# A four-layer graph network on one core: 482 scatters of layer 0's edge pass wait for the batches of the pass

## The chip, the cores and the metric

The kernel runs on one core of one Trainium2 chip. The metric is the device time in microseconds of one execution, the median of several runs. TensorE (PE) has two clock levels, 1.2 and 2.4 GHz; the profile shows the granted clock of a stretch as a share of the higher one. GpSimd is called POOL, VectorE DVE, ScalarE ACT, SyncE SP.

## The reference

A graph of 12,500 nodes and 200,000 edges (sorted by destination `dst`), 128 features, goes through four layers, each on the normalised and rectified output of the one before. Cut to what matters here:

```python
# layer 0: sum of the edge features per destination node, then a two-layer network
recv_agg = segment_sum(edge_attr_128, dst)
x = x + relu(concat(recv_agg, h, u) @ W1 + b1) @ W2 + b2
# layer 1: attention over the incoming edges; s_rel needs a score of every edge
s_rel = (edge_attr_128 @ w_r.T) @ att_w[256:384]
# layer 2: sums over edges in both directions: by col (= dst) and by row (= src)
agg_fwd = segment_sum(w * x[col], row);  agg_bwd = segment_sum(w * x[row], col)
# layer 3: weighted mean over incoming edges, linear maps, layer norm
```

The sums by `src` in layer 2 need the edges in another order, which the kernel works out itself in its first 900 us. A table of keys in device memory (`keyd`) belongs to this order, and is first read back at L2349, in a phase that comes after layer 1.

## The kernel before

The program is a row of phases. Each phase has a block of code for each of the five engines; inside a phase the engines run freely and wait for each other only at semaphores, and all meet at the end of it. Every engine works through its own block strictly in order. The change is in the phase `p_l0` (L1244), layer 0.

**The edge pass.** `edge_pass` (L984) goes over the edges in NR = 391 batches of 512 edges, unrolled by six. For each batch:

- SP loads the batch's edge features, 256 KB, into one of six slots of `XR` (`load_ea`, L1176). The load for batch b waits until `bd` has reached b - 3.
- DVE makes a one-hot selection matrix from the batch's keys (L1005), semaphore `oh`. Then it adds the finished sums of the batch two before into `AREA` (L1044); for this it waits for PE by the semaphore `mmd`. Then it takes the scores of the batch: four products of the edge features with a fixed vector (L1077). The first of the four raises the semaphore `bd` by one. The phase's `bd` is thus the count of batches whose scores have begun.
- PE multiplies features by the selection matrix (L1106, four f32 products that the profile lists as eight matmuls), waits for ACT's copy (`ohb`), counts the edges with four small bf16 matmuls (L1111), and the last of these raises `mmd`.
- ACT copies the selection matrix to bf16 for the count (L1145). It has one buffer for this, so it waits for PE's `mmd` of the batch before. Then it writes the scores of the batch (L1157).

So `mmd` is the one signal from PE on which both ACT and DVE depend in every batch.

```python
i.then_inc(mmd, 1)                            # PE, unit(): i is the last L1111 of the batch
e.wait_ge(mmd, k + 1)                         # ACT, again(s), ahead of L1145
e.wait_ge(mmd, n_mm if ends else n_mm + 2)    # DVE, accumulate(), ahead of L1044
```

**The scatters.** POOL has nothing to do in the edge pass itself. Its block in this phase writes `keyd`: NBP = 482 indirect DMAs (L1256), each of which scatters 128 rows of five numbers from SBUF to rows in device memory. Twelve semaphores `sc` take turns, so at most twelve scatters are on their way at once. Behind them in POOL's queue come the wait for the end of the edge pass (`edone`), two memsets (L1260, L1261) and the additions of the node stage.

Layers 1, 2 and 3 have edge passes as well, in which POOL gathers rows by indirect DMAs (L1214, L1237). Those of layers 2 and 3 use the same `edge_pass` without counts and scores; a gather there waits for the same kind of semaphore `bd` (L1234), here raised by a small memset of DVE (L1047) once PE's `mmd` has come, and may run up to nine batches ahead.

Of the kernel before, what the change touches and what calls it, by code (L numbers as in the profile page):

```python
# [24 lines left out]
def gnn(nc, x, src, dst, ea, ew, u, W1, b1, W2, b2, w, w_r, att, loop_w, Ws, bs, Wd, bd_,  # L25
# [3 lines left out]
    NR = NBF + 1  # L29
# [16 lines left out]
    NBP = 4 * (NCK - 1) + NBT  # L46
# [1129 lines left out]
    def load_ea(p, bd, off=2):  # L1176

        ready = [p.sem(f"ea{s}") for s in range(UN)]

        @p.on("sync")  # L1180
        def _(e):
            v = ea[0:NBF * BE, :].rearrange("(b p r) f -> b p (r f)", p=128, r=4)
            t = ea[NBF * BE:NE, :].rearrange("(p r) f -> p (r f)", r=4)

            def one(b, s):
                e.dma_start(XR[:, s * BE:(s + 1) * BE], v[bass.ds(b, 1)].rearrange("b p k -> (b p) k")).then_inc(ready[s], 16)
            for s in range(UN):
                one(s, s)
            if NIT > 1:
                with e.Fori(1, NIT) as it:  # L1190
                    for s in range(UN):

                        e.wait_ge(bd, (it - 1) * UN + (s + off))
                        one(it * UN + s, s)
            e.wait_ge(bd, (NIT - 1) * UN + off)
            e.dma_start(XR[0:TP, 0:BE], t).then_inc(ready[0], 16)
            for s in range(UN):
                e.wait_ge(ready[s], 16 * (NIT + (s == 0)))
        return ready
# [44 lines left out]
    def p_l0():  # L1244
        p = Phase()
        ready = load_ea(p, p.sem("bd"), 3)
        edge_pass(p, NR, TP, 48, 0, KLD, lambda s: EA[:, s], ready, 16, AB[:, 0, :], count=True, srel=True)
        sc = [p.sem(f"sc{i}") for i in range(12)]

        @p.on("gpsimd")  # L1250
        def _(e):

            for b in range(NBP):
                if b >= 12:
                    e.wait_ge(sc[b % 12], 16 * (b // 12))
                e.indirect_dma_start(keyd, bass.IndirectOffsetOnAxis(ap=SI[:, b:b + 1].bitcast(U32), axis=0),  # L1256
                                     MP[:, 5 * b:5 * b + 5], None).then_inc(sc[b % 12], 16)

            e.wait_ge(p.sem("edone"), 1)
            e.memset(R[32:33, :], M0).then_inc(p.sem("mi"), 1)  # L1260
            e.memset(R[64:65, :], 0.0).then_inc(p.sem("mi"), 1)  # L1261
            e.wait_ge(p.sem("mi"), 2)
            for i in range(12):
                e.wait_ge(sc[i], 16 * ((NBP - 1 - i) // 12 + 1))
        l0_nodes(p)
        p.run()
# [1652 lines left out]
```

## Time and profile before

| | us |
|---|---|
| median of 3 runs | 9834.15 (9824.49 to 9837.78) |
| span of the profiled execution, first to last instruction | 9823.1 |
| layer 0's edge pass: POOL's first scatter starts | 907.76 |
| ... DVE's first batch (L1005) | 923.41 |
| ... POOL's last scatter starts | 1555.80 |
| ... DVE's end signal (L1088) | 2229.64 |

The profiled execution is known by its span; the median of the runs is 11.0 us above it, for what lies around the first and the last instruction and for the spread of the runs.

In the rows further down, a line of a timeline is: start in us, duration in us, engine, source line, operation, what is written and read, how many instructions are merged, and in brackets how long the engine had been idle and what released it. "issue" means nothing that the profile shows; "remote" stands where the profile finds no instruction of this core whose end would have been the release. A line of windows is: the stretch, its length, then for PE, PE's weight loads, DVE, ACT and POOL the busy time and the number of instructions, the granted clock of TensorE, the busy share of the DMA engines and GB/s.

### The profile page before, as it was taken

What the parts mean: (1) busy time and instruction counts of PE and PEld (TensorE: products, weight loads), DVE (VectorE), ACT (ScalarE), POOL (GpSimd) and SP (SyncE); (2) the same over time, 40 slices, a digit from 0 to 9 for tenths busy, and PEclk for the clock granted to TensorE, in tenths of its full rate; (3) what the DMA queues carried; (4) which work ended last, traced back from release to release, by engine and by line L of the source; (5) the groups of instructions that cost most, each with busy time, mean ns of one, the idle gap of its engine ahead of it and who ended that gap; (6) DMA issues with size and microseconds to landing.
All of it is one profiled execution on the core that took longest, in us unless ns stands there. A gap on an engine that the chain in (4) does not pass through costs nothing. (4 is left out here: it accounts for less than half of the span.)

```text
span 9823.1 us, 218886 instructions
## 1 busy us (share of the span) xinstructions
PE 7099.9 (72%) x59894; PEld 6078.6 (62%) x59895; DVE 6196.8 (63%) x20052; ACT 3293.8 (34%) x9071; POOL 4369.4 (44%) x5518
## 2 busy tenths in 40 slices
PE   5943004778967878878878797777797777696777
PEld 5843004765656666666657676667696766696666
DVE  7997004883346666666667676555786556786556
ACT  4722001333432222222223452000560002667785
POOL 0002772001036666666663355566465553465661
PEclk8955557999976666666667899888898887898987
DMA  0001003551123333333333586556686554686553
GB/s 21 2 2 29 10 9 87 150 149 46 38 59 87 86 86 85 87 86 88 87 85 115 198 287 215 164 166 161 245 338 186 164 163 134 253 338 183 166 166 117
DMA packets 640399, 1262.17 MB, mean 128 GB/s; under 512 B 121108, under 2 KB 179132, under 8 KB 639896
## 3 DMA queue, kind: packets, MB, share of 16 engines
q1 hardware_dynamic: 418919, 704.46, 21.3%
q0 software_dynamic: 199040, 544.46, 20.1%
q10 hardware_dynamic: 22196, 10.20, 0.4%
q8 instruction: 129, 2.11, 0.1%
q14 instruction: 115, 0.94, 0.0%
HBM read 780.96 MB, written 477.75 MB: 128 GB/s over the span
## 5 line engine op out<-in xcount | busy, mean ns | idle before, releaser
L1214 POOL DMA_INDIRECT GS<-t1d,KI x1564 | 1479.9, 946 | 1000.3 <-issue 380.3
L1106 PE MATMUL PS<-w,GS 128*128 128x128 f32 x6128 | 902.9, 313 | 319.2 <-DVE w L1005 251.4
L1106 PE MATMUL PS<-w,AREA 128*128 128x128 f32 x6048 | 860.6, 306 | 334.8 <-DVE w L1005 291.1
L1106 PEld LDWEIGHTS PS<-w,GS 128*128 128x128 f32 x6128 | 850.3, 223 | 371.7 <-DVE w L1005 294.1
L1106 PEld LDWEIGHTS PS<-w,AREA 128*128 128x128 f32 x6048 | 808.5, 215 | 385.2 <-DVE w L1005 333.5
L1005 DVE TENSOR_TENSOR w<-PS,KI 128x512 f32<-128x512 f32 x964 | 666.5, 691 | 316.9 <-issue 306.7
L2547 PE MATMUL PS<-AREA 128*128 128x128 bf16 x13392 | 842.7, 220 | 8.4 <-ACT GS L2473 4.6
L2547 PEld LDWEIGHTS PS<-AREA 128*128 128x128 bf16 x13392 | 792.0, 98 | 79.3 <-issue 6.1
L2522 DVE TENSOR_SCALAR AREA<-PS,w 128x1024 bf16<-128x1024 bf16 x558 | 715.9, 1284 | 161.2 <-PE PS L2533 161.2
L2491 POOL TENSOR_TENSOR AREA<-AREA,w 128x192 int32<-128x192 int32 x1116 | 528.3, 504 | 473.1 <-PE PS L2547 296.8
L2473 ACT ACTIVATE GS<-PS 128x1024 f32<-128x1024 f32 x558 | 571.3, 1024 | 315.2 <-PE PS L2547 300.0
L1715 PE MATMUL PS<-w,XR 128*128 128x128 f32 x3128 | 671.8, 381 | 0.0
L1663 ACT ACTIVATE w<-PS,w 128x48 f32<-128x48 f32 x1564 | 341.5, 301 | 941.5 <-PE PS L1658 474.9
L1709 PE MATMUL PS<-w,GS 128*128 128x128 f32 x3128 | 631.4, 370 | 0.0
L1106 PE MATMUL PS<-w,XR 128*128 128x128 f32 x3128 | 508.4, 313 | 165.6 <-DVE w L1005 152.9
L1715 PEld LDWEIGHTS PS<-w,XR 128*128 128x128 f32 x3128 | 577.5, 277 | 56.8 <-issue 45.5
L1237 POOL DMA_INDIRECT GS<-xbuf,KI x484 | 462.6, 956 | 334.0 <-DVE w L1047 226.5
L1709 PEld LDWEIGHTS PS<-w,GS 128*128 128x128 f32 x3128 | 607.5, 287 | 0.7
L1237 POOL DMA_INDIRECT AREA<-xbuf,KI x480 | 458.5, 955 | 303.1 <-DVE w L1047 217.3
L1256 POOL DMA_INDIRECT keyd<-AREA x482 | 487.1, 1011 | 194.0 <-issue 161.9
L1106 PEld LDWEIGHTS PS<-w,XR 128*128 128x128 f32 x3128 | 433.5, 215 | 198.8 <-DVE w L1005 181.7
L1111 PE MATMUL PS<-w,ONB 128*128 128x48 bf16 x1564 | 107.6, 189 | 596.1 <-issue 564.9
(431 smaller groups left out, 14522.1 us busy)
## 6 DMA issues: line engine op xcount, KB each, us to landing
xbuf<-GS SPq DMA_DIRECT2D x558, 512.0 KB
XR<-in_edge_attr SPq DMA_DIRECT2D x780, 256.0 KB
pbuf<-AREA SPq DMA_DIRECT2D x482, 256.0 KB
GS<-t1d,KI POOLq DMA_INDIRECT x1564
AREA<-t2d ACTq DMA_DIRECT2D x121, 64.0 KB
GS<-xbuf,KI POOLq DMA_INDIRECT x484
keyd<-AREA POOLq DMA_INDIRECT x482
AREA<-xbuf,KI POOLq DMA_INDIRECT x480
```

The source lines that it names most:

```text
L1005: return e.tensor_tensor(SEL[s % 3], num.unsqueeze(1).to_broadcast([128, 4, width]), kl.unsqueeze(2).to_broadcast([128, 4, width]), ALU.is ...
L1106: i = e.matmul(PS[:, s % 3, 0:128], feats(s)[0:m, r, 0:D], SELW[s % 3][0:m, width * r:width * r + 128], start=(r == 0), stop=(r == 3))
L1214: e.indirect_dma_start(GS[0:m, s, r, 0:wide], None, table, bass.IndirectOffsetOnAxis(ap=idx[0:m, c:c + 1].bitcast(U32), axis=0)).then_inc( ...
L1237: e.indirect_dma_start(gslot(s), None, buf, bass.IndirectOffsetOnAxis(ap=idx[:, b:b + 1].bitcast(U32), axis=0)).then_inc(ready[s], 16)
L1256: e.indirect_dma_start(keyd, bass.IndirectOffsetOnAxis(ap=SI[:, b:b + 1].bitcast(U32), axis=0), MP[:, 5 * b:5 * b + 5], None).then_inc(sc[ ...
L1663: n = e.activation(U1[i][:, r, :], uv(i)[:, r, :], ACT.Identity, bias=ZC[i][:, r:r + 1])
L1709: n = e.matmul(PS[:, 4 + i, 0:128], GS[0:m, s, r, 0:D], LLW[l][0:m, WD * r:WD * r + 128], start=(r == 0), stop=(r == 3))
L1715: n = e.matmul(PS[:, 4 + i, 128:256], EA[0:m, s, r, :], LLW[l][0:m, WD * r:WD * r + 128], start=(r == 0), stop=(r == 3))
L2473: e.activation(OUT[s % 3], PS[:, 3 + 2 * (s % 2):5 + 2 * (s % 2), :], ACT.Copy).then_inc(ev, 1)
L2491: e.tensor_tensor(WTI[s % UN], TABI[:, bass.ds(held[0][s], 192)], ZI[:, 0:1].to_broadcast([128, 192]), ALU.add).then_inc(wt, 1)
L2522: e.tensor_scalar(OHT[s % 3], PS[:, s % 3, :].bitcast(BF16).rearrange("n (k d) -> n d k", d=2), IPB[:, 0:1], None, ALU.is_equal).then_inc( ...
L2547: i = e.matmul(PS[:, 3 + 2 * (s % 2) + d, 128 * r:128 * r + 128], OHT[s % 3][:, d, 128 * r:128 * r + 128], WT[(2 * s + d) % UN][:, 128 * k ...
```

## The change

Each scatter gets one more wait. The scatter number b waits until `bd` has reached `b * 391 // 482`, which is until the scores of that many batches have begun. The first two scatters (b = 0, 1) wait for nothing, and the last one for 390. Between them each batch frees one scatter, and in 90 of the batches a second one. No instruction is added to any other engine, none is moved, and no DMA changes its size or target.

```diff
@@ -1253,6 +1253,8 @@
             for b in range(NBP):
                 if b >= 12:
                     e.wait_ge(sc[b % 12], 16 * (b // 12))
+                if b * NR // NBP:
+                    e.wait_ge(p.sem("bd"), b * NR // NBP)
                 e.indirect_dma_start(keyd, bass.IndirectOffsetOnAxis(ap=SI[:, b:b + 1].bitcast(U32), axis=0),
                                      MP[:, 5 * b:5 * b + 5], None).then_inc(sc[b % 12], 16)
```

## Rows read from the trace of the kernel before

**Rows 1.** The page, busy tenths in 40 slices of 245.6 us.
```profile
POOL 0002772001036666666663355566465553465661
PEclk8955557999976666666667899888898887898987
```

**Rows 2.** Windows, the edge pass of layer 0 in two stretches.
```profile
923.00:1577.00 654.00, 49.65 (x249) 41.60 (x249) 31.75 (x211) 9.25 (x40) 475.33 (x470) 0.50 0.07 10
1583.00:2229.00 646.00, 492.06 (x4431) 454.82 (x4428) 541.05 (x3689) 209.40 (x738) 0.00 (x0) 0.93 0.51 149
```

**Rows 3.** Groups of instructions, 1000 to 1500 us: count, busy, mean ns, idle before.
```profile
L1256 POOL DMA_INDIRECT keyd<-AREA x370 | 375.8, 1016 | 125.5 <-issue 125.5
...
L1077 DVE CUSTOM_DVE_ANT_0 w<-XR,AREA 128x128 f32<-128x128 f32 x60 | 14.0, 288 | 1.0
...
L1145 ACT ACTIVATE w<-w 128x192 bf16<-128x192 f32 x15 | 5.4, 363 | 497.1 <-remote 497.1
...
L1044 DVE TENSOR_TENSOR AREA<-AREA,PS 128x96 f32 x15 | 3.8, 255 | 476.8 <-remote 476.8
```

**Rows 4.** Timeline, one period of the slow stretch.
```profile
1008.13 0.36 ACT L1145 ACTIVATE w<-w 128x192 bf16<-128x192 f32 x1 [33.14 <-remote]
...
1008.55 0.34 PE L1111 MATMUL PS<-w,ONB 128*128 128x48 bf16 x4 [30.88 <-issue]
1009.21 2.05 PE L1106 MATMUL PS<-w,XR 128*128 128x128 f32 x8 [0.33 <-issue]
...
1041.73 0.36 ACT L1145 ACTIVATE w<-w 128x192 bf16<-128x192 f32 x1 [33.14 <-remote]
1041.83 0.26 DVE L1044 TENSOR_TENSOR AREA<-AREA,PS 128x96 f32 x1 [32.03 <-remote]
```

**Rows 5.** Timeline, ACT and PE at the start of the pass.
```profile
923.88 0.36 ACT L1145 ACTIVATE w<-w 128x192 bf16<-128x192 f32 x1 [5.89 <-DVE w L1005]
...
942.33 0.36 ACT L1145 ACTIVATE w<-w 128x192 bf16<-128x192 f32 x1 [16.93 <-remote]
```

**Rows 6.** Timeline, POOL and ACT where the scatters end.
```profile
1555.80 0.96 POOL L1256 DMA_INDIRECT keyd<-AREA  x1 [0.30 <-issue]
1577.23 0.36 ACT L1145 ACTIVATE w<-w 128x192 bf16<-128x192 f32 x1 [31.04 <-remote]
...
1582.34 0.36 ACT L1145 ACTIVATE w<-w 128x192 bf16<-128x192 f32 x1 [4.65 <-remote]
...
1583.13 0.36 ACT L1145 ACTIVATE w<-w 128x192 bf16<-128x192 f32 x1 [0.34 <-PE PS L1111]
```

**Rows 7.** Groups of instructions, 1583 to 2229 us.
```profile
L1106 PE MATMUL PS<-w,XR 128*128 128x128 f32 x2952 | 463.4, 305 | 153.9 <-DVE w L1005 152.3 <-issue 0.8
...
L1077 DVE CUSTOM_DVE_ANT_0 w<-XR,AREA 128x128 f32<-128x128 f32 x1476 | 342.8, 287 | 25.2
L1145 ACT ACTIVATE w<-w 128x192 bf16<-128x192 f32 x369 | 133.9, 363 | 177.4 <-DVE w L1005 117.5 <-PE PS L1111 57.7 <-issue 2.3
```

**Rows 8.** Timeline of layer 2's first edge pass, one hold of PE's signal.
```profile
6160.12 3.94 PE L1106 MATMUL PS<-w,AREA 128*128 128x128 f32 x32 [1.41 <-DVE w L1005]
...
6164.91 0.95 POOL L1237 DMA_INDIRECT AREA<-pbuf,XR  x1 [0.30 <-issue]
...
6167.08 0.06 DVE L1047 MEMSET w<- 1x1 f32 x1 [0.98 <-DMA GS<-t1d,KI]
```

**Rows 9.** Waits in that pass, 6020 to 6890 us: total, times, longest.
```profile
DVE w L1047 <- PE PS L1106: 152.7, 121, 2.4
```

**Rows 10.** Windows, the edge passes of layer 2 (two), 3 and 1.
```profile
6020.00:6890.00 870.00, 635.06 (x4407) 599.45 (x4405) 517.87 (x1649) 0.00 (x0) 521.57 (x546) 0.88 0.60 164
7370.00:8180.00 810.00, 587.99 (x4276) 553.53 (x4273) 481.40 (x1430) 22.52 (x22) 474.62 (x516) 0.86 0.58 170
8880.00:9640.00 760.00, 544.01 (x3836) 510.73 (x3837) 453.05 (x1445) 603.50 (x1907) 451.92 (x473) 0.89 0.58 164
2860.00:5240.00 2380.00, 1928.28 (x9669) 1483.37 (x9669) 1513.97 (x6568) 610.21 (x2709) 1454.99 (x1538) 0.66 0.33 86
```

## The prediction, made before the changed kernel ran

> **What bounds the kernel now.** I read four views, in this order.
>
> First the slices of the page [rows 1]. POOL is busy 7 tenths in two slices (at about 1000 to 1500 us) while the granted clock of PE stands at 0.5, and right after POOL falls silent the clock goes to 0.9. So something odd happens beside the scatters.
>
> Second the windows of the edge pass [rows 2]. In the 654 us that the scatters take, PE executes 249 instructions; in the 646 us behind it 4431. The groups say it in batches: L1145 runs once per batch, 15 times in 500 us [rows 3] and 369 times in 646 us [rows 7]. A batch takes 33.6 us beside the scatters and 646 / 369 = 1.751 us without them. Half of the pass goes by for 22 batches.
>
> Third, what the slow batches wait for. ACT (L1145) and DVE (L1044) are idle for 497 and 477 of 500 us, and the profile puts the release down to nothing on this core ("remote") [rows 3]. The timeline shows one period [rows 4]. PE's count matmuls of a batch (L1111) end at 1008.55 + 0.34 = 1008.89, PE then does the sums of the next batch, and stands from 1011.26. ACT starts only at 1041.73 and DVE at 1041.83. Both need the one signal that L1111 raises, `mmd`, so it reached them 1041.73 - 1008.89 = 32.84 us late. The period is constant (15 batches in 500 us, idle 33.14 before each). Signals in the other direction are prompt: L1145 starts at 1008.13 and lasts 0.36, PE's L1111 follows at 1008.55. I read this as: while POOL issues scatters without a pause, PE's completion signals are held back, and here they get out only after some 33 us.
>
> That POOL's stream is the cause rests on its two edges. The signals before the first batch pass (ACT at 923.88), at the second batch ACT is idle for 16.93 us [rows 5], and after the last scatter at 1555.80 there are two more late ones, 31.04 and 4.65, and from 1583.13 on none [rows 6].
>
> Fourth, the other edge passes, where POOL gathers and waits for `bd`, as the scatters will. There the signal is held too, but briefly. In layer 2, 32 matmuls (four batches) end at 6164.06; POOL's last gather of that run starts at 6164.91; DVE goes on at 6167.08 [rows 8], 3.0 us after PE's end and 2.17 us after POOL's last issue. POOL had run out of batches that it may gather for, paused, and the signal came out. The longest such wait of DVE for PE in 870 us is 2.4 us, in 121 waits [rows 9]; no 33 us anywhere.
>
> **The change, part by part.**
>
> *The waits themselves.* 480 of 482 scatters get a wait. It is on POOL, which has no other work here: what queues behind is the end of the pass (a memset of one row and the node stage's additions). POOL needs 0.96 + 0.30 = 1.26 us per scatter [rows 6], so 482 / 391 x 1.26 = 1.55 us per batch, less than the 1.751 of a batch: POOL keeps up, and the last scatter (wait for 390) starts one batch before the pass ends. At most the memset begins one scatter later, 1.3 us. The table is first read in a phase behind layer 1, so later scatters cost nobody.
>
> *What the spreading removes.* From DVE's first batch at 923.4 to its end signal at 2229.6 (both in the table of times) are 1306 us for 391 batches. Without any hold it would be 391 x 1.751 = 685 us. That is the most that can be won: 621 us. What is late next is then DVE itself, busy 541 of 646 us [rows 2].
>
> *What the spreading brings.* The scatters now run beside all batches instead of 22. I price three things.
> - Holds of PE's signal. Bounded below by nothing: a batch frees one or two scatters, never four in a row as in rows 8. Bounded above by a full hold in every batch: scores begin, POOL issues, 2.17 us later the signal comes out [rows 8], and about 0.8 us pass until the next scores begin (ACT 0.36, DVE's addition, the first score). That is 3.0 us per batch, 1.2 more than 1.751. The nearest rows are the three passes of layers 2 and 3 [rows 10], with one gather per batch and the same kind of wait. A batch is eight matmuls there: 870 us / 551 = 1.58 us, of which PE is busy 635 / 551 = 1.15, excess 0.43; 810 / 535 = 1.515 against 1.10, excess 0.415; 760 / 480 = 1.585 against 1.135, excess 0.45. I take 0.43 us per batch on top of 1.751, which gives 2.18, times 391 = 852 us. It is an analogy: there the bound is PE, here DVE, and POOL may run further ahead there but needs one DMA per batch against 1.23 here.
> - DMA traffic. The scatters move with 10 GB/s beside loads at 149 GB/s, and the engines' share is 0.07 against 0.51 [rows 2]. SP loads three batches ahead. I cost it at 0; if that cover were gone, it would be at most the 0.07 of 685 us, 48 us.
> - DVE beside POOL. L1077 takes 288 ns beside scatters [rows 3] and 287 without [rows 7]: 0.
>
> The page "SBUF — State Buffer" of the Trainium skill, section "Who interferes with whom", speaks against the change: a DVE instruction with two inputs in SBUF (L1077 is one) and a GpSimd instruction that reads SBUF exclude each other for their whole length. By that rule a scatter would stop the scores. The trace does not agree: 288 against 287 ns. What it would give is the fourth rival.
>
> *The clock.* In the slow stretch it is 0.50, in the fast one 0.93 [rows 2], with PE waiting between batches in both. With short holds I expect 0.8 to 0.9, as in layers 2 and 3 [rows 10]. PE is busy 492 / 369 = 1.33 us per batch at 0.93 [rows 2, 7]; at 0.85 that is 1.46, under DVE's 1.751, and the clock costs nothing. Were it 0.5 throughout, PE would need 2.05 + 0.34 + 0.33 = 2.72 us per batch [rows 4].
>
> *Sum.* 852 - 1306 = -454 us. Against the profiled execution 9823.1 - 454 = 9369; the median lies 11 us above the span, so 9834 - 454 = 9380 us.
>
> **The rivals.**
> 1. *No holds to speak of.* For it: at most two scatters follow each other. Against: 1.26 us issue and 2.17 us until a hold ends overlap from batch to batch at 1.75 us, so POOL's stream may count as unbroken. 9834 - 621 = 9213 us.
> 2. *A hold in every batch, or PE at half clock.* For it: layer 1, with four gathers per batch, has clock 0.66 [rows 10]. Against: layers 2 and 3. 391 x 2.72 to 3.0 = 1064 to 1173 us, so 9592 to 9701 us.
> 3. *The long hold stays (slower).* The place is the same signal, the price some 33.6 us each time. For it: after the last scatter POOL was silent, and still the signal took until 1577.23 and the next until 1582.34 [rows 6]; a pause alone did not free it. The scatters go to device memory and the gathers of layers 1 to 3 come from it, so these may be no guide. It becomes slower than before from (1306 - 685) / 31.8 = 20 long holds on; with one in every batch the pass would take 391 x 33.6 = 13138 us and the kernel about 21670. Against: the first batch passed with a dozen scatters on their way [rows 5], and after a release only one or two scatters follow.
> 4. *DVE and POOL exclude each other.* 482 x 0.958 us = 462 us of scatters on top of 685 us: 1147 us, 9675 us. Against: 288 and 287 ns.
> 5. *The scatters are not the cause* and a slow start stays for another reason: 9834 us. Against: both edges of rows 5 and 6.
>
> The Trainium skill, "DMA: Bandwidth & Descriptors", section "Anatomy of one DMA", says that a DMA's completion can take long above all when it writes to device memory, as the scatters do. No row here shows a scatter's completion. By it a hold would last longer than 2.17 us, which leans to the second rival.
>
> **How the numbers follow.** Forecast, short holds (1.85 to 2.6 us per batch): 0.56. Rival 1: 0.24. Rival 2: 0.11. Rival 3: 0.04. Rival 4: 0.02. Rival 5: 0.03. The forecast's own range is 391 x 1.85 = 723 to 391 x 2.6 = 1017 us, 9251 to 9545. For 8 in 10 I add rival 1 on the low side, down to 9200, and a little of rival 2, up to 9560. A measurement of this kernel tells 0.2% (20 us) from no change. Faster than that are the forecast and rivals 1, 2 and 4: 0.93. The same is rival 5: 0.03. Slower is rival 3: 0.04.
>
> **What would show it.** In the changed profile: no "remote" wait of about 33 us before L1145 and L1044; the pass ends at about 923 + 852 = 1775 us on DVE's end signal; L1256 spread over all of it, its idle time now released by DVE's L1077; ACT's L1145 with waits of 1 to 3 us for PE's L1111, some 100 to 250 of them; clock of the pass 0.8 or more. Rival 1: hardly any such wait and an end near 1610. Rival 2: L1106 at 2.05 us per eight matmuls and clock 0.5. Rival 4: L1077 longer than 290 ns. I am wrong if waits of 30 us stay in number, or if the phases behind layer 0 change by more than the spread of the runs, 13 us.

## The result, and the profile after

The changed kernel takes 9416.92 us (median of 4 runs, 9400.87 to 9427.75) against 9829.32 us of the kernel before in the same comparison: ratio 0.9585, 95% interval 0.9572 to 0.9598. The forecast was 9380 us: 454 us less than before, measured 412. The profiled execution has a span of 9399.2 us, 423.9 less than before.

In the changed kernel all lines behind the edit have moved by two: the scatter is L1258, POOL's memsets are L1262 and L1263. DVE's end signal (L1088) comes at 1816.0 us instead of 2229.6. That is 413.6 of the 423.9 us; the node stage gives 3.2 (layer 1's first gather at 2816.8 before, 2400.0 after) and the rest of the kernel 7.1, which is within the spread of the runs.

The page of the changed kernel, the same two rows as [rows 1], each slice now 235 us:

```profile
POOL 0000555400466666666633556654655551556561
PEclk8965877799666666666678998888998886998887
```

The peak of 7 tenths is gone: the scatters lie over three slices at 5 tenths and one at 4, and the granted clock there is 0.7 to 0.8 instead of 0.5.

Windows of the changed kernel, the whole pass and the node stage with the start of the next phase, to be set against [rows 2]:

```profile
923.00:1816.00 893.00, 619.13 (x4692) 571.56 (x4692) 577.01 (x3913) 193.43 (x782) 468.36 (x480) 0.79 0.47 116
1816.00:2400.00 584.00, 534.39 (x2522) 347.01 (x2522) 192.61 (x1040) 222.37 (x452) 53.03 (x28) 0.95 0.13 35
```

One stretch replaces two. 893 us for 391 batches are 2.28 us each; before, most of the first 22 took 33.6 each and the rest 1.751.

Groups of the changed kernel, 923 to 1816 us, to be set against [rows 3, 7]:

```profile
L1106 PE MATMUL PS<-w,XR 128*128 128x128 f32 x3128 | 578.1, 345 | 118.1 <-DVE AREA L1044 53.2 <-issue 47.2 <-DVE w L1005 14.6
...
L1258 POOL DMA_INDIRECT keyd<-AREA x480 | 468.4, 976 | 432.9 <-DVE w L1077 290.8 <-issue 142.2
...
L1077 DVE CUSTOM_DVE_ANT_0 w<-XR,AREA 128x128 f32<-128x128 f32 x1564 | 363.8, 288 | 26.6
L1145 ACT ACTIVATE w<-w 128x192 bf16<-128x192 f32 x391 | 141.8, 363 | 645.4 <-remote 283.9 <-PE PS L1111 256.0 <-DVE w L1005 76.8
```

POOL is now released by DVE's scores (L1077), as the edit says. L1077 itself lasts 288 ns as before. ACT's idle time is still the largest and still ends with PE's signal, "remote" or L1111. How it is cut up, the waits of the same stretch show (total, times, longest):

```profile
POOL keyd L1258 <- DVE w L1077: 290.8, 149, 14.4
ACT w L1145 <- remote: 283.9, 86, 4.3
ACT w L1145 <- PE PS L1111: 256.0, 229, 2.8
```

No wait of ACT for PE's signal is longer than 4.3 us, where they were 33.14 [rows 4]. The timeline of the changed kernel shows one of the long ones:

```profile
1499.41 0.96 POOL L1258 DMA_INDIRECT keyd<-AREA  x1 [0.30 <-issue]
1500.67 0.96 POOL L1258 DMA_INDIRECT keyd<-AREA  x1 [0.30 <-issue]
1501.02 0.37 PE L1111 MATMUL PS<-w,ONB 128*128 128x48 bf16 x4
1501.93 0.96 POOL L1258 DMA_INDIRECT keyd<-AREA  x1 [0.30 <-issue]
1503.87 0.36 ACT L1145 ACTIVATE w<-w 128x192 bf16<-128x192 f32 x1 [4.02 <-remote]
...
1505.35 0.98 POOL L1258 DMA_INDIRECT keyd<-AREA  x1 [2.46 <-DVE w L1077]
```

PE's last count matmul, which raises `mmd`, ended at 1501.39, inside a run of scatters 1.26 us apart. ACT goes on at 1503.87, 1.94 us after the start of the last of them. The stalled batch had left POOL without a scatter that it might issue, until 1505.35. So the hold starves the stream that causes it, and ends.

### The profile page after: what moved, and what is told of

Same layout as the page of the kernel before. It is cut to its first block and busy times, and to the rows that moved or that the text cites. A ratio compares the mean times of both kernels' runs of the same rounds, so it can differ in the third digit from the quotient of the medians.

```text
span 9399.2 us, 219356 instructions
## 1 busy us (share of the span) xinstructions
PE 7177.7 (76%) x59894; PEld 6153.7 (65%) x59895; DVE 6200.2 (66%) x20052; ACT 3266.3 (35%) x9071; POOL 4357.1 (46%) x5518
## 5 line engine op out<-in xcount | busy, mean ns | idle before, releaser
L1106 PE MATMUL PS<-w,GS 128*128 128x128 f32 x6128 | 882.1, 308 | 333.9 <-DVE w L1005 277.3
L1106 PE MATMUL PS<-w,AREA 128*128 128x128 f32 x6048 | 884.6, 312 | 317.4 <-DVE w L1005 257.4
L1106 PEld LDWEIGHTS PS<-w,GS 128*128 128x128 f32 x6128 | 828.9, 218 | 386.2 <-DVE w L1005 320.4
L1106 PEld LDWEIGHTS PS<-w,AREA 128*128 128x128 f32 x6048 | 832.8, 221 | 368.6 <-DVE w L1005 297.9
L1005 DVE TENSOR_TENSOR w<-PS,KI 128x512 f32<-128x512 f32 x964 | 666.6, 691 | 318.0 <-issue 307.4
L1258 POOL DMA_INDIRECT keyd<-AREA x482 | 470.5, 976 | 465.4 <-DVE w L1077 290.8
L1717 PE MATMUL PS<-w,XR 128*128 128x128 f32 x3128 | 674.9, 383 | 0.0
L1106 PE MATMUL PS<-w,XR 128*128 128x128 f32 x3128 | 578.1, 345 | 118.1 <-DVE AREA L1044 53.2
L1711 PE MATMUL PS<-w,GS 128*128 128x128 f32 x3128 | 631.4, 370 | 0.0
L1717 PEld LDWEIGHTS PS<-w,XR 128*128 128x128 f32 x3128 | 580.2, 278 | 57.5 <-issue 46.8
L1711 PEld LDWEIGHTS PS<-w,GS 128*128 128x128 f32 x3128 | 608.4, 287 | 0.5
L1106 PEld LDWEIGHTS PS<-w,XR 128*128 128x128 f32 x3128 | 507.1, 246 | 135.8 <-DVE w L1005 72.4
L1005 DVE TENSOR_TENSOR w<-PS,XR 128x512 f32<-128x512 f32 x558 | 385.9, 692 | 179.6 <-issue 174.4
```

The costliest lines, as they stand in the source:

```text
L1005: return e.tensor_tensor(SEL[s % 3], num.unsqueeze(1).to_broadcast([128, 4, width]), kl.unsqueeze(2).to_broadcast([128, 4, width]), ALU.is ...
L1106: i = e.matmul(PS[:, s % 3, 0:128], feats(s)[0:m, r, 0:D], SELW[s % 3][0:m, width * r:width * r + 128], start=(r == 0), stop=(r == 3))
L1711: n = e.matmul(PS[:, 4 + i, 0:128], GS[0:m, s, r, 0:D], LLW[l][0:m, WD * r:WD * r + 128], start=(r == 0), stop=(r == 3))
L1717: n = e.matmul(PS[:, 4 + i, 128:256], EA[0:m, s, r, :], LLW[l][0:m, WD * r:WD * r + 128], start=(r == 0), stop=(r == 3))
```

## The experiments

Twelve runs in five sessions after that of the result, and the sessions turned out not to be alike. The kernel before, run in each of them, took 8269, 8265, 9829, 9904 and 9834 us. In the first two no recorded signal `mmd` of layer 0's pass is more than 0.02 us behind the end of its matmul, in the other three many are. I call them sessions without and with holds. The two profiles of this case belong to the second kind. The record gives a chip number for each session: 11, 2, 2, 13 and 12. The same number, 2, stands for one without holds and, a quarter of an hour later, for one with them, so, if the number means one chip, it is a state rather than a fixed trait; what sets it is not known. Every run on record has a granted clock, which is read from the profiler's records, so none tells whether holds occur without that recording.

### First session (without holds): four kernels

**All scatters behind the node stage.** The loop of scatters is moved to the end of the phase.

```diff
+            e.wait_ge(p.sem("edone"), 1)
+            e.memset(R[32:33, :], M0).then_inc(p.sem("mi"), 1)
+            e.memset(R[64:65, :], 0.0).then_inc(p.sem("mi"), 1)
+            e.wait_ge(p.sem("mi"), 2)
+        l0_nodes(p)
+
+        @p.on("gpsimd")
+        def _(e):
             for b in range(NBP):
                 if b >= 12:
                     e.wait_ge(sc[b % 12], 16 * (b // 12))
...
-            e.wait_ge(p.sem("edone"), 1)
-            e.memset(R[32:33, :], M0).then_inc(p.sem("mi"), 1)
-            e.memset(R[64:65, :], 0.0).then_inc(p.sem("mi"), 1)
-            e.wait_ge(p.sem("mi"), 2)
...
-        l0_nodes(p)
         p.run()
```

> Base: the kernel before. All 482 scatters are taken out of layer 0's edge pass and issued by POOL at the end of the phase, behind the node stage; the pass has no indirect DMA at all. Theory (the scatters hold back PE's signals, and that is all they cost the pass): 391 batches at 1.75 us, as in rows 7, so the pass ends near 1620 us instead of 1816, no wait for a remote signal is longer than 1 us, and the granted clock in the pass is 0.9 or more. The scatters then follow one another for 482 x 1.0 to 1.3 us = 480 to 630 us behind the node stage, so the time is 9417 - 200 + 550 = about 9770 (9690 to 9850). Rival (the 0.53 us per batch above 1.75 in the changed kernel come from something else in the first 650 us of the pass, its loads or its keys): the pass still takes 2.2 us or more per batch and ends after 1780 us.

Measured: 8818.7 us (4 runs) against 8268.85, ratio 1.0667 (1.0649 to 1.0684). The pass ends (L1088) at 1609.0 us. No signal is held here, so the run does not test its theory. The scatters run from 2127.6 to 2735.2, and layer 1's first gather starts at 2754.5, where the changed kernel has it at 2196.0 in the second session. Scatters that nothing covers cost their length less what the end of the node stage hides, 550 us.

**Pauses.** Ahead of every fourth scatter POOL waits for the four before to land.

```diff
             for b in range(NBP):
-                if b >= 12:
-                    e.wait_ge(sc[b % 12], 16 * (b // 12))
+                if b and b % 4 == 0:
+                    for i in range(b - 4, b):
+                        e.wait_ge(sc[i % 12], 16 * (i // 12 + 1))
```

> Base: the kernel before, with no wait for the batches. POOL waits ahead of every fourth scatter until the four before have landed; the scatters stay bunched at the start of the pass. Theory (a held signal goes out as soon as none of POOL's indirect DMAs is on its way or being issued, some 1.7 us behind the last issue): with a pause behind each four, PE's signal comes once per group of four, every 5 to 8 us, in place of every 33.6 us. So about 121 batches or more pass while the scatters last, the waits of about 33 us are gone, and the pass ends near 2000 us (1900 to 2130), the whole near 9600. Rival (only the tie to the batches, or the end of the stream, frees a signal): the waits of 33 us stay, in 600 to 900 us of scatters only 20 to 30 batches run, and the pass ends at 2230 us or later.

Measured: 8439.91 us (one run). The pass ends at 1607.5, but the last scatter starts only at 1818.0, and the memsets and the node stage wait for it: 171 us. The run says nothing of holds.

**Behind PE's own signal.**

```diff
-                if b * NR // NBP:
-                    e.wait_ge(p.sem("bd"), b * NR // NBP)
+                if b * NR // NBP:
+                    e.wait_ge(p.sem("mmd"), b * NR // NBP + 2)
```

> Base: the changed kernel. The same number of scatters per batch, but each waits for PE's own count of finished batches (mmd reaches b*391//482 + 2) in place of the batch's scores having begun, so that POOL issues right behind PE's signal and the hold of some 1.7 us falls into PE's next batch of 1.75 us. Theory (a hold costs only what of it lies behind the next signal): the 391 batches lose less than now, 2.0 us per batch in place of 2.28, pass 110 us shorter, 9310 (9250 to 9400). Rival (the number of scatters per batch counts, not where they lie: any issue in a batch delays its signal by the same): same as the changed kernel within 20 us. Second rival: POOL's start waits for the held signal as well, each scatter is late and a second one of the same batch follows; slower by up to 100 us.

Measured: 8266.61 us (10 runs), ratio 1.000 (0.999 to 1.001). The pass ends at 1608.6. Where the holds are absent the place of a scatter within the batch means nothing, and what it would do with holds was not run again: this stays open.

**Gathers in place of the scatters.** 482 gathers of 128 rows of 512 bytes from the input `x`, the scatters at the end of the phase. The end signal of the pass waits for the gathers as well (not shown), and stands at L1090 here.

```diff
-                e.indirect_dma_start(keyd, bass.IndirectOffsetOnAxis(ap=SI[:, b:b + 1].bitcast(U32), axis=0),
-                                     MP[:, 5 * b:5 * b + 5], None).then_inc(sc[b % 12], 16)
+                e.indirect_dma_start(GF[:, 128 * (b % 12):128 * (b % 12) + 128], None, x,
+                                     bass.IndirectOffsetOnAxis(ap=IDX[:, b:b + 1].bitcast(U32), axis=0)
+                                     ).then_inc(sc[b % 12], 16)
```

> Base: the kernel before. In the edge pass POOL issues 482 gathers of 128 rows of 512 bytes from an input in place of the 482 scatters, one behind the other and at most twelve on their way; the scatters themselves come at the end of the phase, as in the kernel with late scatters. It tells whether the hold belongs to writes into device memory or to the stream of indirect DMAs as such. Theory (the stream): waits of tens of us for PE's signal while the gathers last, 33 us if the period does not depend on the direction, 15 to 30 batches run meanwhile, and the pass ends 450 us or more later than with no indirect DMA, near 2150 to 2250. Rival (writes): no wait over 5 us, the pass ends near 1620 to 1850.

Measured: 8823.3 us (one run), the pass ends at 1609.1. Again nothing on holds. What the session shows is that the kernel before loses nothing to its scatters there.

### Second session (without holds): the change itself

> The changed kernel itself, once more beside the kernel before, in another session on the chips. In the session of the four experiments before this one, the kernel before took 8269 us in place of 9834, and no wait for PE's signal was longer than 1.2 us, with the scatters in the pass as without them. Theory (the hold of PE's signals belongs to the chip or the machine on which the first profiles were taken, and the change gains by nothing but shortening it): where the kernel before takes some 8270 us, the changed kernel takes the same within 0.2% (8250 to 8290), its pass ends near 1607 as without any scatters; where the kernel before takes some 9830, it takes 9417 again (ratio 0.957 to 0.960). Rival (the change also gains something of its own, without holds): ratio below 0.998 at 8270 too. Second rival (the waits cost something where there are no holds): ratio above 1.002.

Measured: 8265.58 us (10 runs) against 8265.12 (13 runs), ratio 1.000 (0.999 to 1.001). First the window of this pass, then the waits of ACT in it:

```profile
923.00:1607.00 684.00, 521.92 (x4681) 483.15 (x4682) 573.07 (x3902) 221.53 (x780) 468.89 (x480) 0.93 0.62 150
```

```profile
ACT w L1145 <- DVE w L1005: 133.5, 275, 5.9
ACT w L1145 <- PE PS L1111: 58.8, 109, 1.2
```

The same 480 scatters beside the same batches, and the pass takes 684 us, 1.75 per batch, as the stretch without scatters in [rows 7]. ACT never waits for "remote" and at most 1.2 us for PE. So the scatters' DMA traffic, their SBUF reads and POOL's work cost the pass nothing. The change gains by shortening the holds alone; without them it is worth nothing, and costs nothing.

### Third session (with holds): where the holds are

**All scatters behind the node stage, again.** The edit is the one above.

> All 482 scatters at the end of the phase, none in the edge pass, run again to meet a chip with holds. Where the kernel before takes some 9830 us on the chip (holds there). Theory (scatters hold PE's signals, and nothing else slows the pass on such a chip): the pass ends near 1607 as on the chips without holds, and the whole is 9417 - 209 + 550 = 9760 (9680 to 9850). Rival (a chip with holds is slower in this pass whatever POOL does): the pass ends after 1700. Where the kernel before takes some 8270 us: 8819 as before, and nothing new.

Measured: 9808.52 us against 9829.1 (one run each), within the range. The window of the pass:

```profile
923.00:1608.00 685.00, 522.93 (x4692) 483.95 (x4692) 574.29 (x3911) 222.34 (x782) 0.00 (x0) 0.93 0.51 148
```

685 us, the pace of the sessions without holds. In a session with holds the pass is slow only for what POOL issues beside it. The rest of the gain is eaten by the scatters in the open (2126.6 to 2773.3).

This trace also shows what a hold is made of. Scatters run beside the last groups of the node stage too, and there PE goes one step at a time. First PE and its weight loads, then ACT where it waits for the signal behind four matmuls:

```profile
2180.78 0.37 PE L1454 MATMUL PS<-AREA,GS 128*128 128x128 f32 x1 [2.43 <-issue]
2182.18 0.29 PEld L1454 LDWEIGHTS PS<-AREA,GS 128*128 128x128 f32 x1 [2.51 <-issue]
2183.58 0.37 PE L1454 MATMUL PS<-AREA,GS 128*128 128x128 f32 x1 [2.43 <-issue]
...
2344.59 0.44 ACT L1479 ACTIVATE GS<-PS,w 128x212 f32<-128x212 f32 x1 [10.76 <-remote]
2355.80 0.44 ACT L1479 ACTIVATE GS<-PS,w 128x212 f32<-128x212 f32 x1 [10.76 <-remote]
```

Weight load and matmul take turns, 1.40 us apart, so a matmul starts every 2.80 us; between 2146 and 2493 us, 61 matmuls start 2.79 or 2.80 us behind the one before, and in the first session's run of this kernel not one does. The signals follow the same count. Behind four matmuls they come every 11.20 us, which is 4 x 2.80. The signal behind 64 matmuls of L1454 is recorded at 2579.77, 179.20 us behind the one before it (2400.57), and DVE waits 174.7 us for it: 64 x 2.80 is 179.20. A batch of the edge pass has twelve matmuls, and 12 x 2.80 is the 33.6 us of [rows 4]. So the 33.6 us are, by these three counts, no time of their own: beside an unbroken stream PE's work is completed at one matmul per 2.80 us. PE runs some way ahead of that (the signal behind the matmul that ended at 2223.15 was recorded at 2310.97), so in the short batches only the signal is late. No run changed the number of matmuls of a batch to test this.

**Pauses, again.**

> A wait for the landing of four scatters ahead of every fourth, no wait for the batches, run again to meet a chip with holds. Where the kernel before takes some 9830 us. Theory (a held signal goes out as soon as no indirect DMA of POOL is on its way or being issued): the waits of some 33 us are gone, a signal of PE comes once per group of four scatters or oftener, 120 batches or more run while the scatters last, the pass ends at 1850 to 2130, the whole at 9450 to 9730. Rival (only the tie to the batches or the end of the stream frees a signal): 33 us waits stay and the pass ends at 2230 or later, the whole at 9834 or more. Where the kernel before takes some 8270 us: 8440 again, since the scatters end after the pass and the two memsets wait for them.

Measured: 9413.52 us; the pass ends at 1819.0. The waits of the pass, then a piece of the timeline:

```profile
ACT w L1145 <- PE PS L1111: 283.7, 231, 3.0
ACT w L1145 <- remote: 253.8, 81, 4.7
```

```profile
1102.20 0.99 POOL L1257 DMA_INDIRECT keyd<-AREA  x1 [0.30 <-issue]
...
1103.49 0.96 POOL L1257 DMA_INDIRECT keyd<-AREA  x1 [0.30 <-issue]
...
1104.75 0.96 POOL L1257 DMA_INDIRECT keyd<-AREA  x1 [0.30 <-issue]
...
1106.71 0.36 ACT L1145 ACTIVATE w<-w 128x192 bf16<-128x192 f32 x1 [3.36 <-remote]
...
1107.62 0.96 POOL L1257 DMA_INDIRECT keyd<-AREA  x1 [1.91 <-DMA keyd<-AREA]
```

ACT goes on 1.96 us after the start of the last scatter of the group, 0.9 us before POOL does. This kernel has no tie between scatters and batches at all, and gets the whole gain of the changed one (pass end 1819.0 against 1816.0, 9413.5 against 9416.9 us). The theory holds, its rival (only the tie, or the end of the stream) falls, and my ranges, 1850 to 2130 for the pass end and 9450 to 9730 for the whole, were both missed on the fast side.

**Half of the scatters in the node stage.** 232 in the pass, 250 in the node stage, where PE works without a gap and raises a signal (`ph`) with each pair of its long matmuls.

```diff
+        def scatter(e, b, sem, n):
+            if b >= 12:
+                e.wait_ge(sc[b % 12], 16 * (b // 12))
+            if n:
+                e.wait_ge(sem, n)
...
-            for b in range(NBP):
...
+            for b in range(NBP - 10 * NG):
+                scatter(e, b, p.sem("bd"), b * NR // (NBP - 10 * NG))
...
                                 ).then_inc(xb, 1)
+                for k in range(10):
+                    scatter(e, NBP - 10 * NG + 10 * g + k, ph, 8 * g + min(k, 7) + 1)
```

> Base: the changed kernel. 232 scatters in the pass (0.59 per batch in place of 1.23) and 250 in the node stage, ten per group of nodes, each behind one of PE's signals there (ph). Where the kernel before takes some 9830 us. Theory (each scatter in the pass costs the pass about (892.6 - 684) / 482 = 0.43 us by the hold behind it, and in the node stage, where PE is busy without a gap, a hold of 1.7 us is covered by its two buffers): the pass is 108 us shorter, the node stage up to 60 us longer, 9340 (9290 to 9420). Rival (the node stage cannot cover the holds, 250 x 0.43 = 108 us come back there): 9417, the same as the changed kernel. Where the kernel before takes some 8270 us: 8270 plus what the node stage loses, 0 to 20.

Measured: 9193.72 us, against 9829.1 a ratio of 0.935. Windows of the pass and of the node stage, and the group of the scatters in the latter:

```profile
923.00:1610.00 687.00, 520.01 (x4692) 479.05 (x4692) 574.71 (x3914) 219.88 (x782) 226.13 (x232) 0.94 0.56 149
1610.00:2204.00 594.00, 537.32 (x2522) 349.02 (x2522) 214.01 (x1039) 221.96 (x452) 293.41 (x277) 0.94 0.15 37
```

```profile
L1255 POOL DMA_INDIRECT keyd<-AREA x250 | 240.2, 961 | 258.8 <-PE PS L1454 228.5 <-issue 30.3
```

It is outside the expected range, on the fast side: the pass is at its full pace (687 us), not 108 but 206 us shorter than in the changed kernel, and the node stage takes 594 instead of 584 us. The cost is not in proportion to the number of scatters.

### Fourth session (with holds, the kernel before at 9904 us)

**The same kernel, timed.**

> The kernel with 232 scatters in the pass and 250 in the node stage, timed. In a session with holds (the kernel before at some 9830 us): 9194 again (9170 to 9215), which is 2.4% below the changed kernel. In a session without holds (the kernel before at some 8270): 8270 to 8290; theory: the node stage hides them there too, so within 0.2% of the kernel before. Rival: POOL, which also adds in the node stage, is late by the scatters ahead of its additions, and the time is 10 to 40 us above.

Measured: 9280.51 us (4 runs, 9277.23 to 9296.59) against 9904.36 (7 runs), ratio 0.9374 (0.9358 to 0.939). The session is slower than the one before it, by 0.8% for the kernel before and 0.9% for this one, so the absolute time missed its range; the ratio stands. It beats the changed kernel (0.9585). The two were not run in one session, but the intervals are far apart: 0.9374 / 0.9585 = 0.978. In a session without holds it was not run.

**The same number, two at a time.**

```diff
-                scatter(e, b, p.sem("bd"), b * NR // (NBP - 10 * NG))
+                scatter(e, b, p.sem("bd"), b // 2 * 2 * NR // (NBP - 10 * NG))
```

> Base: the split kernel. The same 232 scatters in the pass and 250 in the node stage, but in the pass two at a time: both of a pair wait for the batch of the first, so that they are issued 1.3 us apart and pairs follow each 3.4 batches, in place of one scatter every 1.7 batches. Number and bytes are the same. Only a session with holds tells. Theory (a signal of PE is held only when an indirect DMA is issued while the one before is less than some 1.6 us old, and it goes out 1.45 us behind the last issue; a lone scatter holds nothing): each pair holds the signal for up to 2.7 us, 116 pairs cost 0.3 to 0.9 us each, the pass ends 35 to 105 us later than 1612, the whole at 9230 to 9300. Rival (the number of scatters per batch decides, and under about one per batch nothing is held): 9194, as with the split kernel.

Measured: 9285.43 us; the pass ends at 1618.3 against 1611.4 with single scatters. First ACT's waits for PE with single scatters, then with pairs, then a pair in the timeline:

```profile
ACT w L1145 <- PE PS L1111: 95.8, 144, 1.6
```

```profile
ACT w L1145 <- PE PS L1111: 161.8, 202, 2.4
```

```profile
1106.41 0.98 POOL L1255 DMA_INDIRECT keyd<-AREA  x1 [3.69 <-DVE w L1077]
...
1107.60 0.26 PE L1111 MATMUL PS<-w,ONB 128*128 128x48 bf16 x4
1107.69 0.96 POOL L1255 DMA_INDIRECT keyd<-AREA  x1 [0.30 <-issue]
...
1109.30 0.36 ACT L1145 ACTIVATE w<-w 128x192 bf16<-128x192 f32 x1 [1.18 <-PE PS L1111]
```

PE's signal of 1107.86 came 1.44 us late, 1.6 us after the second of the pair had started. The holds behaved as the theory says. I set the moments at which the trace records the signal `mmd` against the ends of the last L1111 before them. Of 373 recorded signals in each, 45 came over 0.3 us late with single scatters (41 us in sum), 96 with pairs (112 us), none over 1.55 us. With pairs, where PE's matmul ended within 1.2 us behind the second of two scatters under 1.4 us apart, its signal was late 83 times in 86. But my price for it was wrong: 116 pairs cost the pass 7 us and not 35 to 105. So signals up to 1.5 us late are nearly absorbed by the batches. The likely reason, not tested by itself, is that in the free pass ACT waits for DVE (L1005) more than for PE.

**Gathers, again.**

> 482 gathers of 128 rows of 512 bytes in place of the scatters in the pass, one behind the other with at most twelve on their way, the scatters at the end of the phase; run again to meet a session with holds. Theory (the hold belongs to the stream of indirect DMAs, whatever their direction): waits of some 33 us while the gathers last, the pass ends near 2150 to 2250 and the whole at 10350 to 10450. Rival (it belongs to writes into device memory): the pass ends near 1607, the whole at 9810 as with the late scatters. Between them: the gathers hold for less than 33 us and the pass ends between.

Measured: 10497.09 us against 9904.36; the pass ends at 2230.6, as the theory says, and the whole is above its range in this slower session. ACT's copy is L1147 here. The window beside the gathers, the group of ACT's copies at 1000 to 1500 us, and a step of the timeline:

```profile
923.00:1560.00 637.00, 49.40 (x248) 41.50 (x248) 31.17 (x210) 9.25 (x40) 483.71 (x471) 0.50 0.21 56
```

```profile
L1147 ACT ACTIVATE w<-w 128x192 bf16<-128x192 f32 x15 | 5.4, 362 | 497.9 <-remote 265.4 <-issue 232.5
```

```profile
1116.74 0.36 ACT L1147 ACTIVATE w<-w 128x192 bf16<-128x192 f32 x1 [33.14 <-remote]
1116.83 0.26 DVE L1044 TENSOR_TENSOR AREA<-AREA,PS 128x96 f32 x1 [32.04 <-remote]
```

248 PE instructions where [rows 2] have 249, 15 batches in 500 us as in [rows 3], the same 33.14 us. Gathers into SBUF of 512 bytes a row hold as scatters of 20 bytes a row into device memory do. For these two forms direction and bytes don't matter, the unbroken stream of indirect DMAs does; the rival "writes" falls.

### Fifth session (with holds, the kernel before at 9834 us): one scatter per batch

```diff
-            for b in range(NBP - 10 * NG):
-                scatter(e, b, p.sem("bd"), b * NR // (NBP - 10 * NG))
+            for b in range(NBP - 4 * NG):
+                scatter(e, b, p.sem("bd"), b * NR // (NBP - 4 * NG))
...
-                for k in range(10):
-                    scatter(e, NBP - 10 * NG + 10 * g + k, ph, 8 * g + min(k, 7) + 1)
+                for k in range(4):
+                    scatter(e, NBP - 4 * NG + 4 * g + k, ph, 8 * g + 2 * k + 1)
```

> Base: the split kernel, with 382 scatters in the pass (0.98 per batch, each behind its own batch's scores) and 100 in the node stage, four per group of nodes. Only a session with holds tells, and times are set against the kernel before there: split is 0.937 of it, the changed kernel 0.9585. Theory (a lone scatter holds nothing, one issued less than 1.6 us behind the one before starts a hold that lasts until 1.45 us behind the last issue; a hold of up to 1.5 us is absorbed by the batch's slack, longer ones are not): most distances between batches are 1.1 to 1.6 us with one of 2.7 in about six, so scatters one per batch come less than 1.6 us apart five times in six, runs of up to five build holds of 2 to 5 us, and the pass ends 60 to 150 us behind the split kernel's 1610, so at 1670 to 1760; ratio 0.943 to 0.953. Rival (the cost follows the number above some count per pass, (382 - 232) / (482 - 232) = 0.6 of the 209 us at most, evenly): 125 us. Second rival (at one per batch nothing is held, since the scatters keep the batches' own distance of 1.75 us): pass ends at 1610 to 1625, ratio 0.937.

Measured: 9306.92 us, ratio 0.9464; the pass ends at 1711.7, 102 us behind the split kernel's 1609.9. Its window and its waits:

```profile
923.00:1712.00 789.00, 576.84 (x4696) 534.87 (x4695) 576.33 (x3915) 196.41 (x782) 374.10 (x382) 0.84 0.51 131
```

```profile
ACT w L1145 <- PE PS L1111: 256.7, 236, 2.7
ACT w L1145 <- remote: 144.1, 55, 3.5
```

Within the theory's range, and the second rival (nothing is held at one per batch) falls. An even price per scatter above 232 would give 125 us here, which one run does not tell apart from 102, so this rival stands. The pairs show that the distance between scatters decides which signals are late, and in this kernel all 57 signals over 1.55 us late came behind the third or fourth scatter of a run less than 1.65 us apart. The number alone does not set the length of the pass: 482 scatters end it at 2229.6 us in one stream and at 1816.0 spread. Whether, once they are spread, it follows the runs or the number above some count is not shown.

The kernels with holds, side by side (scatters less than 1.65 us behind the one before, and late signals, counted from the start times and recorded signals in the traces; up to 9% of the 391 signals are not recorded):

| scatters in the pass | close behind another | signals over 1.55 us late | longest | pass ends |
|---|---|---|---|---|
| none (third session) | 0 | 0 | 0.0 | 1608.2 |
| 232, single (third session) | 59 of 231 | 0 | 1.5 | 1609.9 |
| 232, single (fourth session) | 57 of 231 | 0 | 1.5 | 1611.4 |
| 232, pairs | 114 of 231 | 0 | 1.5 | 1618.3 |
| 382, one per batch | 208 of 381 | 57 | 3.0 | 1711.7 |
| 482, groups of four with pauses | 361 of 481 | 76 | 4.2 | 1819.0 |
| 482, the change | 306 of 481 | 85 | 4.5 | 1816.0 |
| 482, the kernel before | 469 of 481 | 21 | 32.8 | 2229.6 |

The pass is longer where signals over 1.55 us late appear, and grows with their number and length.

## Why the prediction was right, and where it was off

**What bounds the kernel.** Right, and now shown from both sides: with no indirect DMA in the pass, or in a session without holds, a batch takes 1.75 us; with a stream of other indirect DMAs in place of the scatters most of the batches beside it take 33.6 us again. That PE's completion signals are held is what every run with holds shows; what in the machine holds them is not.

**The waits cost nothing.** Right. POOL kept up (its last scatter starts at 1809.9, 6 us ahead of the end signal), and the second session has the ratio 1.000.

**What the spreading removes.** 621 us were called the most that can be won. That was right: the split kernel's pass of 687 us is the 685 forecast for a pass without holds, and DVE is what it then waits for.

**The price of the short holds** is the term that was mis-sized: 0.43 us per batch forecast, (892.6 / 391) - 1.75 = 0.53 measured, with the 892.6 us from 923.4 to 1816.0. It makes the pass 41 us longer than forecast, and the time 37 us. The range, 1.85 to 2.6 us per batch, held. The analogy with layer 2 had two errors. The 0.43 was taken over PE's busy time, not over the free pace of that pass. The session without holds gives that pace, first pass of layer 2:

```profile
4930.00:5670.00 740.00, 590.50 (x4468) 532.79 (x4468) 529.19 (x1682) 0.00 (x0) 531.27 (x556) 0.98 0.72 198
```

That is 4468 / 8 = 558 batches at 740 / 558 = 1.33 us against 1.58 with holds [rows 10], so the holds cost 0.25 there and the rest of the 0.43 is not theirs. With 0.25 the sum would have been 782 us, 110 short of the 892.6: the two errors had opposite signs, and that 0.43 came within 41 us is in part luck. The other error is that there one gather per batch is issued, here 1.23 scatters, which come in runs (93 of the 176 runs in the trace are of three to five scatters less than 1.65 us apart) and make the next hold longer. The long holds of 3 to 4.5 us are what I had excluded ("never four in a row"): a batch frees one or two, but a late POOL catches up.

**DMA traffic and DVE beside POOL** at 0: both right, by the second session (684 us with the scatters beside, L1077 at 288 ns). With that the fourth rival has fallen. The rule of the Trainium skill, "SBUF — State Buffer", section "Who interferes with whom", does not show in a DVE instruction beside POOL's issues of indirect DMAs in these traces. The same section adds, as inferred, that making a DMA's descriptors needs the write side of the shared ports, which an instruction with two inputs does not take. The 288 ns agree with that.

**The clock.** Forecast 0.8 to 0.9, measured 0.79 in the pass, just outside. PE's busy time went to 619 / 391 = 1.58 us per batch, under DVE's 1.75 as argued. With the same work and no holds it is 0.93, so the lower clock goes with PE's longer waits. That it does not set the time is argued from these shares, and no run tests it.

**The rivals.** First (no holds to speak of, 9213): fallen for this kernel, and met by the split kernel, whose 0.9374 of 9834 is 9219. Second (a hold in every batch, 9592 up): fallen, 315 waits of ACT for PE's signal in 391 batches, most of them short, though this is more than the 100 to 250 that the prediction gave as its sign. Third (the long hold stays since a pause does not free it): fallen, the longest wait is 4.3 us, and the pauses of the third session free the signal. What spoke for it [rows 6], two late signals behind the last scatter, is not explained: the last packet of the scatters starts at 1557.5 in the trace, and PE's signal is recorded at 1577.2, almost as late as if the stream had gone on. And what the prediction set against it, that "the first batch passed", was no evidence: ACT at 923.88 was released by DVE [rows 5] and needed no signal of PE, and PE's first signal, behind a matmul that ended at 926.07, was recorded at 942.30. Fifth (scatters not the cause): fallen.

The Trainium skill, "DMA: Bandwidth & Descriptors", section "Anatomy of one DMA", warns of long completions of writes into device memory. The kernel with pauses now has rows for it: the scatters land 2.1, 2.2 and 3.8 us (least, median, most) behind their issue, so none is slow enough to hold a signal for 33 us. In the timeline above the scatter of 1104.75 and PE's signal do come out together, both first recorded at 1106.69. But in the kernel with pairs each of the 96 late signals is recorded 0.17 us or more before the first record of the last scatter's landing, 0.5 us in the median. So a hold does not wait for that landing. The longer holds go with longer runs of issues, as the table says.

## What to carry to other kernels

Where an engine's signals come late with "remote" and PE has ended long before, look at what POOL issues at that time. If it is a stream of indirect DMAs back to back, 1.26 us apart here, thin it out or break it up: a tie to the batches and a pause behind every fourth gave the same gain here. Put the surplus in a stage that hides it; the node stage took 250 scatters for 10 us more. The same 482 scatters cost the pass 621 us in one stream and 207 spread. Whether their number or their distance sets what is left is not settled. Time such a change in several sessions: the same edit was worth 4.1% in one and nothing in another.

## What the runs showed of the hardware that I had not expected

- The same two kernels take 8265 and 8266 us in one session and 9829 and 9417 in another. Of the 1133 us between the changed kernel's two profiles 207 lie in layer 0's pass, 438 between the first and the last gather of layer 1 (2403.8 against 1965.6 us), and the rest, some 490, behind that, in layers 2 and 3 for the most part: their three stretches of gathers take 881, 771 and 765 us against 724, 612 and 613.
- With holds, PE beside an unbroken stream of scatters or gathers is completed at one matmul with its weight load per 2.80 us (third session), which is 33.6 us for a batch of twelve and 179.2 us for 64; it is the same 33.6 us for 20 and for 512 bytes a row. A stream that breaks up sooner lets the signal go, for 106 of 134 late signals of the changed kernel and 104 of 151 of the one with pauses 0.9 to 2.1 us after the start of the last issue; my 1.45 us was too exact. Why 2.80, why the signals stay late for 21 us behind the end of a long stream [rows 6], and how long a stream must be for it, is open.
- A lone indirect DMA does little, but not nothing. Take the matmuls that end within 1.4 us behind a scatter with none in the 1.9 us before it. In the split kernel their signals were over 0.3 us late 0 times in 58 (third session) and 3 in 60 (fourth), with pairs 7 in 52, with one per batch 25 in 106, in the changed kernel 18 in 86; most of them by 0.5 us.
- In the edge pass DVE's signals to POOL and ACT's to PE were prompt in the timelines above, also inside a hold [rows 4]; only PE's were seen to be late. DVE is not quite untouched: in the third session's kernel with all scatters behind the node stage its instructions L1541 and L1543 start 0.7 to 1.4 us apart at 2586 to 2590 us, and 0.2 to 0.3 us apart in the first session's.
